# A six-layer attention and gated-MLP kernel: the rounding of the value output, its low part, and the weight remainders change engines and places

## The chip, the cores and the metric

The kernel runs on one core of a Trainium2 chip. The metric is the time of one execution in microseconds, as the median of several runs. The core has five engines that run their own instruction streams in order and wait for each other by semaphores: TensorE (PE in the rows; its weight loads are PEld), VectorE (DVE), ScalarE (ACT), GpSimd (POOL) and SyncE (SP), which issues the DMAs here.

## What is computed

`x` has 16 sequences of 256 tokens with 128 channels. A layer norm and a small causal linear attention are added to it first. Then, on another layer norm of it, come six layers, and most of the time lies there. Each layer is

```python
for i in range(DEPTH):                      # 6
    x = attn_layer(shift_tokens(x), Wqkv[i], q_scale[i], k_scale[i], Wo[i]) + x
    x = ffn_layer(shift_tokens(x), ln_g[i], ln_b[i], W1[i], b1[i], W2[i], b2[i]) + x

def attn_layer(x, Wqkv, qs, ksc, Wo):
    q, k, v = split(x @ Wqkv)               # 16 heads of 64
    q = l2norm(q) * qs;  k = l2norm(k) * ksc
    q, k = rotary(q, scale), rotary(k, 1 / scale)
    out = local_attention(q, k, v)          # windows of 32, looking one window back
    return out @ Wo

def ffn_layer(x, g, bln, W1, b1, W2, b2):
    a, gate = split((layernorm(x) * g + bln) @ W1 + b1)
    return a * gelu(gate) @ W2 + b2
```

All of it is float32.

## The kernel before, in words

**Split products.** A projection with near-float32 accuracy is made of three matmuls on rounded (fp32r) operands: `hi*hi + hi*lo + lo*hi`. For this each operand is rounded (`_hi`, by ScalarE) and the remainder `raw - hi` formed (`_lo`). It concerns the input `xs`, the value output `OT` (the attention's output, transposed), the normed `xn`, and the weights `wqkv`, `wo`, `w1`.

**Slots.** The six layers run as one software pipeline. A slot handles one sequence ("batch") of one layer, and there are 16 slots a layer, 96 in all. In slot n the projections (`proj`, eight chunks of 512 columns for q and k, and `v`, four) are made for batch n (lag 0), rope, transposes (`tr`) and attention scores for n-1 (lag 1, written with one '), the end of attention and the output projection for n-2 (lag 2, ''), the MLP for n-3 (lag 3, '''). `pipeline` calls `body` for each slot, `run_slots` runs through one engine's row of the table `ORDER` and calls the step for each word. So the order on each engine is written out by hand in that table, and only semaphores relate the engines. Names of steps: `proj` and `v` (projections), `sums` (squares' sums), `rsqrt` (ten small VectorE instructions that give the reciprocal roots for the q and k norms and for the layer norm at once), `add` and `norm` (GpSimd: sum of the rope parts, multiplication with the reciprocal root), `tr` (transpose into `b_trA`, copied to qT or kT), `qk` (scores into `b_sim`), `mk` (mask put back), `pt` (transpose of the probabilities), `pv` (product with V), `ot` (transpose of its result), `wo`, `x1`, `mean`, `var`, `ln` (layer norm), `xl` (GpSimd: `xn_lo`), `w1.0` to `w1.2`, `w2`. The four units of attention of a batch have numbers 0 to 3.

**The value output.** `pt` and `ot` share one PSUM bank, `b_trB` (its order is `TRB_ORDER`; `trB_free` is TensorE's wait for it). After `ot.u` ScalarE copies the bank to `OT` (L920, step `ot`), and that frees the bank. A second ScalarE step, `oh` (L930), rounds `OT` into `OT_hi`, and GpSimd (step `ol`, L1022) forms `OT_lo = OT - OT_hi`. `wo` (L743) waits for all four `ot_lo_done`.

**Layer edges.** At an edge the weights change under the running pipeline. ScalarE rounds the raw weights (`w_a`, L824, in three thirds of q, k and v; `w_cs`, from L969, for `wo`, the layer norm, `w1` and the rest), GpSimd forms the remainders (`w_a` L1043, together with the scaled rotary table `rotary_scaled`; `w_low`, L1031 for `wo` and L1034 for `w1`). `EDGE` says behind which word of the table a third is done; the words `wc` and `wd` stand in the table and act only in the slots in which their weights change. In the table `wd.0''` and `wd.1'''` are GpSimd's last words, behind `norm.5`. SP loads the raw weights of the next layer at once, by 20 DMAs (`load_weights` from `loads`), ahead of the slot of the layer's fourth batch; its other DMAs in a slot are `xres`, two for `xraw`, the store of x, and ten that place V.

## Time and profile before

| | us |
|---|---|
| median of 3 runs | 3533.07 |
| lowest, highest | 3528.24, 3535.49 |
| the profiled execution | 3529.75 |
| its span | 3527.9 |

The mean granted TensorE clock of the profiled execution is 0.974 of full speed. The busy shares are: TensorE 93%, its weight loads 77%, VectorE 85%, ScalarE 77%, GpSimd 70%. Matmuls are pipelined and their ends are modelled, so a TensorE that shows as busy is not one at its peak. Shares are means over stages: a prologue of some 360 us with the linear attention, the pipeline, and its short end. "Releaser" in a row is who ended a wait, "issue" is time in which an engine waited for nothing that the profile shows.

### The profile page before, as it was taken

The page shows a single profiled execution, that of the slowest core. Times are in us where ns is not written, and L with a number is a line of the kernel's source. Part 1 is how long each engine was busy: PE and PEld are TensorE (multiplying, and loading weights), DVE is VectorE, ACT ScalarE, POOL GpSimd, SP SyncE. Part 2 cuts the span into 40 slices and gives each one's busy share as a digit, 9 for nine tenths or more (in the row PEclk, how much of TensorE's full clock was granted, in tenths as well). Part 3 has the DMA queues.
Part 4 walks back from the last instruction along what each step waited for, and adds up shares of the span by engine and source line. Part 5 has one row for each costly group of instructions (what it writes and reads, how often), then busy time and mean ns, then how long its engine had stood idle before and what let it go on. Part 6 is the DMA issues. An engine that isn't in the chain of part 4 may idle for free.

```text
span 3527.9 us, 154148 instructions
## 1 busy us (share of the span) xinstructions
PE 3292.8 (93%) x64868; PEld 2708.3 (77%) x64868; DVE 3003.9 (85%) x5981; ACT 2708.9 (77%) x5023; POOL 2460.6 (70%) x2131
## 2 busy tenths in 40 slices
PE   5867999999899999899999899999899999999997
PEld 2325788887788887788887788887788888788886
DVE  7988898888788888788898788988788988888984
ACT  2015788888788888788888788888788888788884
POOL 1435678778677778677777677777677777777772
PEclk9998999999999999999999999999999999999998
DMA  2002333333333333433332433332423332323333
GB/s 86 12 27 52 91 84 80 69 77 82 90 85 71 70 85 76 95 74 68 85 84 63 105 71 75 85 82 59 107 65 84 84 76 66 76 66 85 84 80 83
DMA packets 186849, 268.07 MB, mean 76 GB/s; under 512 B 31671, under 2 KB 89909, under 8 KB 185397
## 3 DMA queue, kind: packets, MB, share of 16 engines
q1 hardware_dynamic: 186164, 258.24, 32.6%
q8 instruction: 516, 8.45, 1.0%
q14 instruction: 169, 1.38, 0.1%
HBM read 22.30 MB, written 4.19 MB: 8 GB/s over the span
## 4 chain that ended last, share of the span: by engine, by line
PE 61%; DVE 14%; issue 12%; POOL 8%; ACT 3%; SPq 1%; DVEq 0%; DMA 0%; POOLq 0%; ACTq 0%
PE bank L681 9%; PE bank L694 8%; PE obank L728 6%; PE bank L657 6%; PE bank L659 4%; PE bank L658 4%; PE bank L738 4%; PE bank L791 3%; POOL qn L1014 3%; POOL qn L1008 3%; PE bank L746 2%; PE bank L747 2%; PE bank L748 2%; PE bank L782 2%; PE bank L784 2%
## 5 line engine op out<-in xcount | busy, mean ns | idle before, releaser
L1014 POOL TENSOR_TENSOR qn<-qn,rinv 128x512 f32<-128x512 f32 x768 | 785.6, 1043 | 663.3 <-DVE rinv L1282 663.3
L1008 POOL TENSOR_TENSOR qn<-ropec,ropes 128x512 f32<-128x512 f32 x768 | 990.6, 1313 | 67.8 <-DVE ropes L1234 67.8
L879 ACT ACTIVATE sq<-bank 128x512 f32<-128x512 f32 x768 | 460.0, 599 | 179.1 <-PE bank L659 162.2
L1233 DVE TENSOR_TENSOR ropec<-bank,rots 128x512 f32<-128x512 f32 x768 | 524.2, 683 | 62.9 <-ACT sq L879 56.4
L1242 DVE TENSOR_REDUCE ss<-sq 128x8 f32<-128x512 f32 x768 | 520.1, 678 | 52.4 <-ACT sq L879 46.2
L1234 DVE TENSOR_TENSOR ropes<-bank,rots 128x512 f32<-128x512 f32 x768 | 522.5, 680 | 0.0
L1022 POOL TENSOR_TENSOR OT_lo<-OT,OT_hi 128x512 fp32r<-128x512 f32 x384 | 488.6, 1284 | 31.2 <-ACT OT_hi L930 30.7
L681 PE MATMUL bank<-ident,qn 128*128 128x128 f32 x3072 | 483.0, 280 | 12.6 <-ACT qT L897 7.1
L694 PE MATMUL bank<-kT,qT 64*32 64x64 f32 x24576 | 422.9, 218 | 10.5 <-ACT bank L903 8.0
L694 PEld LDWEIGHTS bank<-kT,qT 64*32 64x32 f32 x24576 | 360.7, 107 | 84.5 <-issue 32.0
L681 PEld LDWEIGHTS bank<-ident,qn 128*128 128x128 f32 x3072 | 340.5, 141 | 96.9 <-issue 45.5
L657 PE MATMUL bank<-wqkv_hi,xs_hi 128*128 128x512 f32 x768 | 361.8, 471 | 16.5 <-POOL wqkv_lo L1043 9.3
L728 PE MATMUL obank<-V,PT 64*32 64x65 f32 x24576 | 352.3, 227 | 8.7 <-issue 8.2
L914 ACT ACTIVATE PT<-bank 128x512 f32<-128x512 f32 x384 | 230.3, 600 | 127.9 <-PE bank L704 127.8
L728 PEld LDWEIGHTS obank<-V,PT 64*32 64x32 f32 x24576 | 289.0, 106 | 45.0 <-issue 44.3
L1288 DVE TENSOR_REDUCE mx<-bank 128x8 f32<-128x512 f32 x384 | 262.4, 683 | 70.2 <-PE bank L694 69.7
L659 PE MATMUL bank<-wqkv_hi,xs_lo 128*128 128x512 f32 x768 | 306.6, 399 | 0.0
L658 PE MATMUL bank<-wqkv_lo,xs_hi 128*128 128x512 f32 x768 | 305.2, 397 | 0.0
L1304 DVE TENSOR_TENSOR On<-obank,rs 128x512 f32<-128x512 f32 x384 | 265.5, 691 | 13.5 <-DVE rs L1299 0.2
L1293 DVE TENSOR_TENSOR Pr<-bank,mx 128x512 f32<-128x512 f32 x384 | 265.5, 691 | 13.2
L920 ACT ACTIVATE OT<-bank 128x512 f32<-128x512 f32 x384 | 231.2, 602 | 36.7 <-POOL OT_lo L1022 31.3
L897 ACT ACTIVATE qT<-bank 128x512 f32<-128x512 f32 x384 | 229.6, 598 | 37.9 <-PE bank L681 36.9
(155 smaller groups left out, 7802.3 us busy)
## 6 DMA issues: line engine op xcount, KB each, us to landing
V<-Vt SPq DMA_DIRECT2D x576, 260.0 KB
V<-Vt SPq DMA_DIRECT2D x192, 130.0 KB
V<-Vt SPq DMA_DIRECT2D x192, 65.0 KB
xres<-X SPq DMA_DIRECT2D x96, 128.0 KB, 2.1
X<-x SPq DMA_DIRECT2D x96, 128.0 KB, 2.1
wqkv_raw<-L_ffn_Wqkv SPq DMA_DIRECT2D x6, 1536.0 KB
xraw<-X SPq DMA_DIRECT2D x97, 64.0 KB, 2.1
xraw<-X SPq DMA_DIRECT2D x97, 63.8 KB, 2.0
```

The source lines that it names most:

```text
L657: pe.matmul(o, xs_hi[:, rows], wqkv_hi[:, cols], start=True, stop=False)
L659: pe.matmul(o, xs_lo[:, rows], wqkv_hi[:, cols], start=False, stop=True).then_inc(proj_full.sem, 1)
L681: mm = pe.transpose(b_trA[:, j * P:(j + 1) * P], qn[:, c, j * P:(j + 1) * P], ident[:])
L694: mm = pe.matmul(b_sim[w * WIN:(w + 1) * WIN, col:col + 2 * WIN], qT[64 * par:64 * par + 64, m, q0:q0 + WIN], kT[64 * par:64 * par + 64, m ...
L728: mm = pe.matmul(obank[w * WIN:(w + 1) * WIN, slot, j * 65:j * 65 + 65], PT[rows, u % 2, j * P + w * WIN:j * P + (w + 1) * WIN], V[rows, w ...
L879: act.activation(sq[:, c % 2, :], b_proj[n % 2][:], ACT.Square).then_inc(squared.sem, 1)
L1008: pool.tensor_tensor(qn[:, c, :], ropec[:, c % ROPE_RING, :], ropes[:, c % ROPE_RING, :], ALU.add).then_inc(rope_sum.sem, 1)
L1014: pool.tensor_tensor(heads8(qn[:, c, :]), heads8(qn[:, c, :]), rinv[:, 8 * c:8 * c + 8].unsqueeze(2).broadcast_to([P, 8, DH]), ALU.mult).t ...
L1022: pool.tensor_tensor(OT_lo[unit], OT[:, u % 2], OT_hi[unit].bitcast(F32), ALU.subtract).then_inc(ot_lo_done.sem, 1)
L1233: dve.tensor_tensor(halves(ropec[:, c % ROPE_RING, :]), raw, table(t, 2 * kind), ALU.mult)
L1234: dve.tensor_tensor(halves(ropes[:, c % ROPE_RING, :]), raw[:, :, ::-1, :], table(t, 2 * kind + 1), ALU.mult).then_inc(roped.sem, 1)
L1242: dve.tensor_reduce(ss[:, 8 * c:8 * c + 8], heads8(sq[:, c % 2, :]), AX.X, ALU.add).then_inc(ss_done.sem, 1)
```

## The change

The value output. ScalarE no longer copies the bank to `OT`; its step `ot` rounds the bank straight into `OT_hi`. The step `oh` is gone. `ol` has moved from GpSimd to VectorE and subtracts `OT_hi` from the bank itself. So the bank is free when `ot_lo_done` is raised, and TensorE's `trB_free` waits for that.

The weights. `wd.1'''` stands behind `add.3` and `wd.0''` behind `add.7`, both ahead of GpSimd's norms of the slot. The thirds have other places in `EDGE`, and the rotary table is scaled with the second third instead of the first. SP loads the weights in six parts, in the slots of six successive batches (g = 4 to 9), each ahead of the placement of V, and the Wqkv load is in three DMAs, so there are 22.

The table. All four rows are new. TensorE's slot now begins at `proj.0`; `w1.0` and `pv.2` stand at the end of the slot before, which is the same place in the cycle. Six norms in front of the slot's end have become four, with `norm.4` to `norm.7` in the next slot. `ln.0` stands ahead of `v.3` instead of behind it on TensorE, and `xn`, `xn_hi` (the step `ln`) are ahead of `v.3` on ScalarE.

```diff
     "pool": """
-        add.0 norm.6' norm.7' ol.0'' add.1 add.2 ol.1'' ol.2'' ol.3'' add.3 add.4 add.5 add.6 norm.0 norm.1
-        xl.0'' norm.2 add.7 norm.3 norm.4 norm.5 wd.0'' wd.1''' """,
+        add.0 norm.4' norm.5' norm.6' add.1 add.2 norm.7' add.3 wd.1''' add.4 add.5 add.6 add.7 wd.0'' norm.0 norm.1 xl.0''
+        norm.2 norm.3 """,
...
-        EDGE = {"act": {"last": {("proj", 7): 0, ("v", 1): 1}, "first": {("proj", 1): 2}},
-                "pool": {"last": {("add", 6): 0, ("norm", 5): 1}, "first": {("add", 2): 2}}}
+        EDGE = {"act": {"last": {("proj", 6): 0, ("proj", 7): 1}, "first": {("proj", 1): 2}},
+                "pool": {"last": {("add", 6): 0, ("add", 7): 1}, "first": {("add", 4): 2}}}
...
+                         load=(l + 1, g - 4) if 4 <= g < 10 else None)
...
+                if load is not None:
+                    loads(*load)
                 if has_a:
                     place_v(n)
...
                 if k == "pt":
                     pe.wait_ge(pt_copied.sem, pt_copied.at(batch, n + 1))
                 else:
-                    pe.wait_ge(ot_copied.sem, ot_copied.at(batch, n + 1))
+                    pe.wait_ge(ot_lo_done.sem, ot_lo_done.at(batch, n + 1))
...
             def b_ot(b, u):
                 t, par = UNIT[u]
                 act.wait_ge(trB_full.sem, trB_full.at(b, TRB_ORDER.index(("ot", u)) + 1))
-                act.wait_ge(ot_lo_done.sem, ot_lo_done.at(b, u - 1) if u >= 2 else ot_lo_done.at(b - 1, u + 3))
-                act.activation(OT[:, u % 2], b_trB[:].rearrange("p (j q) -> p j q", j=4),
-                               ACT.Copy).then_inc(ot_copied.sem, 1)
-
-            def b_oh(b, u):
-                t, par = UNIT[u]
-                act.wait_ge(ot_copied.sem, ot_copied.at(b, u + 1))
                 if u == 0:
 
                     act.wait_ge(c_full.sem, c_full.at(b - 1, 1))
                 unit = (slice(0, P), slice(4 * par, 4 * par + 4), slice(t * P, t * P + P))
-                act.activation(OT_hi[unit], OT[:, u % 2], ACT.Copy).then_inc(ot_hi_done.sem, 1)
+                act.activation(OT_hi[unit], b_trB[:].rearrange("p (j q) -> p j q", j=4), ACT.Copy).then_inc(ot_copied.sem, 1)
...
-                if k == 0:
+                if k == 1:
                     pool.wait_ge(roped.sem, roped.at(layer * NB, 8))
                     rotary_scaled(pool).then_inc(rots_done, 1)
...
+            def b_ol(b, u):
+                t, par = UNIT[u]
+                dve.wait_ge(ot_copied.sem, ot_copied.at(b, u + 1))
+                unit = (slice(0, P), slice(4 * par, 4 * par + 4), slice(t * P, t * P + P))
+                dve.tensor_tensor(OT_lo[unit], b_trB[:].rearrange("p (j q) -> p j q", j=4), OT_hi[unit].bitcast(F32),
+                                  ALU.subtract).then_inc(ot_lo_done.sem, 1)
```

The cycle of the other engines, from `proj.0`, is now, in the table's words. TensorE: `proj.0 tr.1' pt.3'' proj.1 w1.1''' tr.2' proj.2 tr.3' ot.1'' w1.2''' tr.4' proj.3 pv.3'' tr.5' ot.2'' proj.4 tr.6' w2.0''' tr.7' ot.3'' proj.5 proj.6 qk.0' wo.0'' qk.1' proj.7 v.0 mean.0'' pt.0' qk.2' var.0'' v.1 v.2 pt.1' pv.0' qk.3' pt.2' ln.0'' v.3 pv.1' tr.0 ot.0' w1.0'' pv.2'`. VectorE, from the previous batch's `qk.3''`: `qk.3'' pv.1'' xs.0 ol.0'' pv.2'' w1.0''' proj.0 sums.0 sums.1 w1.1''' proj.1 proj.2 sums.2 w1.2''' ol.1'' pv.3'' proj.3 ol.2'' sums.3 proj.4 w2.0''' sums.4 ol.3'' sums.5 qk.0' proj.5 proj.6 x1.0'' qk.1' sums.6 mean.0'' proj.7 sums.7 var.0'' qk.2' rsqrt.0 pv.0' ln.0''`. ScalarE, at the turn of the slot: `pt.2' v.2 ln.0'' v.3 | xs.0 qk.3'' tr.0' ot.0'' w1.0''' proj.0 tr.1'`.

Two places in the instruction order. On VectorE, behind the rsqrt and up to the first rope of the next batch, it is before (`rs` and `On` are the step `pv`, `mx` and `Pr` the step `qk`, `hm` is `w1`, `ropec` and `ropes` are `proj`):

```order
568 L1304 TENSOR_TENSOR On<-obank,rs 128x2x4x64
569 L1325 TENSOR_TENSOR lnt<-dlt,bank 128x256
570 L1288 TENSOR_REDUCE mx<-bank 128x8
571 L1293 TENSOR_TENSOR Pr<-bank,mx 128x512
572 L1299 RECIPROCAL rs<-obank 128x8
573 L1304 TENSOR_TENSOR On<-obank,rs 128x2x4x64
574 L1221 TENSOR_TENSOR xs_lo<-xraw,xs_hi 128x256
575 L1299 RECIPROCAL rs<-obank 128x8
576 L1304 TENSOR_TENSOR On<-obank,rs 128x2x4x64
577 L1330 SCALAR_TENSOR_TENSOR hm<-bank,vec,gel 128x256
578 L1233 TENSOR_TENSOR ropec<-bank,rots 128x512
579 L1234 TENSOR_TENSOR ropes<-bank,rots 128x512
```

and on VectorE now:

```order
648 L1328 TENSOR_TENSOR lnt<-dlt,bank 128x256
649 L1291 TENSOR_REDUCE mx<-bank 128x8
650 L1296 TENSOR_TENSOR Pr<-bank,mx 128x512
651 L1302 RECIPROCAL rs<-obank 128x8
652 L1307 TENSOR_TENSOR On<-obank,rs 128x2x4x64
653 L1224 TENSOR_TENSOR xs_lo<-xraw,xs_hi 128x256
654 L1218 TENSOR_TENSOR OT_lo<-bank,OT_hi 128x4x128
655 L1302 RECIPROCAL rs<-obank 128x8
656 L1307 TENSOR_TENSOR On<-obank,rs 128x2x4x64
657 L1333 SCALAR_TENSOR_TENSOR hm<-bank,vec,gel 128x256
658 L1236 TENSOR_TENSOR ropec<-bank,rots 128x512
659 L1237 TENSOR_TENSOR ropes<-bank,rots 128x512
```

The first of the four subtractions has come in between `xs_lo` and `pv.2`; the others stand further on, behind `w1.2`, `proj.3` and `sums.4`.

On GpSimd, at the layer edge at which `w1` changes, it is before:

```order
247 L1008 TENSOR_TENSOR qn<-ropec,ropes 128x512 x4
248 L1014 TENSOR_TENSOR qn<-qn,rinv 128x512 x2
249 L1026 TENSOR_TENSOR xn_lo<-xn,xn_hi 128x256
250 L1014 TENSOR_TENSOR qn<-qn,rinv 128x512
251 L1008 TENSOR_TENSOR qn<-ropec,ropes 128x512
252 L1014 TENSOR_TENSOR qn<-qn,rinv 128x512 x3
253 L1034 TENSOR_TENSOR w_lo<-w_raw,w_hi 128x682
254 L1008 TENSOR_TENSOR qn<-ropec,ropes 128x512
```

and now:

```order
194 L1010 TENSOR_TENSOR qn<-ropec,ropes 128x512
195 L1016 TENSOR_TENSOR qn<-qn,rinv 128x512 x3
196 L1010 TENSOR_TENSOR qn<-ropec,ropes 128x512 x2
197 L1016 TENSOR_TENSOR qn<-qn,rinv 128x512
198 L1010 TENSOR_TENSOR qn<-ropec,ropes 128x512
199 L1030 TENSOR_TENSOR w_lo<-w_raw,w_hi 128x682
200 L1010 TENSOR_TENSOR qn<-ropec,ropes 128x512 x4
201 L1016 TENSOR_TENSOR qn<-qn,rinv 128x512 x2
202 L1022 TENSOR_TENSOR xn_lo<-xn,xn_hi 128x256
```

`w_lo` stood behind the six norms that follow the rsqrt, and stands now among the rope sums ahead of them.

## Rows read from the trace of the kernel before

**Rows 1.** The page: busy time, share of the span and instructions of each engine.

```profile
PE 3292.8 (93%) x64868; PEld 2708.3 (77%) x64868; DVE 3003.9 (85%) x5981; ACT 2708.9 (77%) x5023; POOL 2460.6 (70%) x2131
```

**Rows 2.** Busy us of each engine in one interior slot, granted clock, DMA share, GB/s.

```profile
1599.30:1631.20 31.90, 31.79 (x670) 26.88 (x670) 28.54 (x60) 27.50 (x52) 24.00 (x21) 1.00 0.34 78
```

**Rows 3.** Waits of the whole span: engine, line, releaser; us, times, longest.

```profile
PEld bank L768 <- DVE rinv L1282: 47.5, 90, 2.5
...
PE bank L782 <- POOL w_lo L1034: 33.9, 5, 6.8
...
PE bank L657 <- POOL wqkv_lo L1043: 9.3, 5, 1.9
...
SPq L488 <- PE obank L728: 1764.4, 95, 28.2
```

**Rows 4.** TensorE's timeline: the first and the last ln between which 91 slots lie.

```profile
433.53 0.71 PE L768 MATMUL bank<-ident,rinv 128*128 128x128 f32 x4
...
3448.45 0.71 PE L768 MATMUL bank<-ident,rinv 128*128 128x128 f32 x4
```

**Rows 5.** Windows as in rows 2, at one layer edge.

```profile
1434.00:1441.00 7.00, 7.00 (x93) 6.03 (x94) 2.58 (x6) 4.00 (x7) 0.00 (x0) 0.65 0.01 2
...
1455.00:1462.00 7.00, 7.00 (x219) 6.06 (x218) 6.66 (x14) 4.95 (x11) 2.06 (x2) 1.00 1.05 305
...
1469.00:1476.00 7.00, 6.10 (x118) 5.49 (x110) 3.45 (x5) 3.63 (x7) 5.91 (x6) 0.50 0.12 36
```

**Rows 6.** Waits at the same edge, from 1466 to 1504.

```profile
PE bank L674 <- issue: 2.6, 1, 2.6
```

**Rows 7.** ScalarE's timeline in one slot: start, length, instruction (us).

```profile
1536.49 0.60 ACT L954 ACTIVATE xn<-lnt,vec 128x256 f32<-128x256 f32 x1 [0.39 <-issue]
1537.18 0.42 ACT L957 ACTIVATE xn_hi<-xn 128x256 fp32r<-128x256 f32 x1
1537.51 0.40 ACT L873 ACTIVATE xs_hi<-xraw 128x256 fp32r<-128x256 f32 x1
...
1538.75 0.59 ACT L920 ACTIVATE OT<-bank 128x512 f32<-128x512 f32 x1
1539.23 0.63 ACT L908 ACTIVATE Pr<-Pr 128x512 f32<-128x512 f32 x1
1539.88 1.28 ACT L948 ACT_TABLE_LOAD   x1
1541.17 0.47 ACT L948 ACTIVATE gel<-bank,vec 128x256 f32<-128x256 f32 x1
1541.54 0.59 ACT L897 ACTIVATE qT<-bank 128x512 f32<-128x512 f32 x1
1542.02 0.60 ACT L879 ACTIVATE sq<-bank 128x512 f32<-128x512 f32 x1
```

**Rows 8.** VectorE's timeline in the same slot.

```profile
1534.95 0.23 DVE L1282 SCALAR_TENSOR_TENSOR rinv<-bank,rinv 128x66 f32<-128x66 f32 x1
1535.10 0.20 DVE L1299 RECIPROCAL rs<-obank 128x8 f32<-128x8 f32 x1
...
1535.98 0.42 DVE L1325 TENSOR_TENSOR lnt<-dlt,bank 128x256 f32<-128x256 f32 x1
1537.04 0.69 DVE L1288 TENSOR_REDUCE mx<-bank 128x8 f32<-128x512 f32 x1 [0.64 <-PE bank L694]
...
1538.38 0.20 DVE L1299 RECIPROCAL rs<-obank 128x8 f32<-128x8 f32 x1
...
1539.21 0.48 DVE L1221 TENSOR_TENSOR xs_lo<-xraw,xs_hi 128x256 fp32r<-128x256 f32 x1
...
1541.68 0.48 DVE L1330 SCALAR_TENSOR_TENSOR hm<-bank,vec,gel 128x256 f32<-128x256 f32 x1
1542.65 0.69 DVE L1233 TENSOR_TENSOR ropec<-bank,rots 128x512 f32<-128x512 f32 x1 [0.49 <-ACT sq L879]
1543.26 0.68 DVE L1234 TENSOR_TENSOR ropes<-bank,rots 128x512 f32<-128x512 f32 x1
```

More of the change, by code:

```diff
@@ L316, in pipeline @@
             for l in range(DEPTH - 1):
-                loads and loads(l + 1)
                 for g in range(3, NB):
                     body(l * NB + g + 1, g, (0, 1, 2, 3), None, {2: l, 3: l},
-                         edge=("last", l + 1) if g == NB - 1 else None)
+                         edge=("last", l + 1) if g == NB - 1 else None,
+                         load=(l + 1, g - 4) if 4 <= g < 10 else None)
                 body(l * NB + NB + 1, 0, (0, 1, 2, 3), l + 1, {2: l, 3: l}, edge=("first", l + 1))
@@ L335, in build, with run_slots @@
                      "dve": {"x1": (0, 1), "mean": (2, 3), "rsqrt": (4,), "ln": (5, 6)}}
-        EDGE = {"act": {"last": {("proj", 7): 0, ("v", 1): 1}, "first": {("proj", 1): 2}},
-                "pool": {"last": {("add", 6): 0, ("norm", 5): 1}, "first": {("add", 2): 2}}}
-        def run_slots(steps, engine, n, g, lags, layer, c_layers, conv_c=None, end=0, edge=None):
+        EDGE = {"act": {"last": {("proj", 6): 0, ("proj", 7): 1}, "first": {("proj", 1): 2}},
+                "pool": {"last": {("add", 6): 0, ("add", 7): 1}, "first": {("add", 4): 2}}}
+        def run_slots(steps, engine, n, g, lags, layer, c_layers, conv_c=None, end=0, edge=None, load=None):
             for kind, i, lag in order(engine):
@@ L461, in _ @@
-            load_weights(0)
+                one = slice(layer, layer + 1)
+                if part < 3:
+                    cols = slice(part * INNER, (part + 1) * INNER)
+                    sp.dma_start(wqkv_raw[:, cols], Wqkv[one, :, cols].rearrange("l p n -> p (l n)")).then_inc(w_in_sem, 16)
+                elif part == 3:
+                    for slot in range(2):
+                        for par in range(2):
+                            src = Wo[one].rearrange("l (j s r p) n -> s r p (l j) n", j=4, s=2, r=2)[slot, par]
+                            sp.dma_start(wo_raw[slot * 64:slot * 64 + 64, 4 * par:4 * par + 4, :], src).then_inc(w_in_sem, 16)
+                elif part == 4:
+                    sp.dma_start(w1_raw[:], W1[one].rearrange("l p n -> p (l n)")).then_inc(w_in_sem, 16)
+                    for j, (f0, n) in enumerate(FFB):
+                        sp.dma_start(w2_raw[0:n, j, :], W2[one, f0:f0 + n].rearrange("l p n -> p (l n)")).then_inc(w_in_sem, 16)
+                    sp.dma_start(qks_raw[:, 0, :], q_scale[one].broadcast_to([P, DH])).then_inc(w_in_sem, 16)
+                    sp.dma_start(qks_raw[:, 1, :], k_scale[one].broadcast_to([P, DH])).then_inc(w_in_sem, 16)
+                else:
+                    col(0, ln_g[one].rearrange("l p -> p l"))
+                    col(1, ln_b[one].rearrange("l p -> p l"))
+                    col(2, b2[one].rearrange("l p -> p l"))
+                    for j, (f0, n) in enumerate(FFB):
+                        col(3 + j, b1[one, f0:f0 + n].rearrange("l p -> p l"), n)
+                        col(6 + j, b1[one, FF + f0:FF + f0 + n].rearrange("l p -> p l"), n)
@@ L463, in _ @@
+            for part in range(6):
+                load_weights(0, part)
             sp.wait_ge(ln_cp, 8)
@@ L503, in place_v, with body @@
                     move(half, 0, 0, P - WIN, slice(1, 2), WIN)
-            def body(n, g, lags, layer, c_layers, conv_c=None, end=0, edge=None):
+            def body(n, g, lags, layer, c_layers, conv_c=None, end=0, edge=None, load=None):
                 has_a, has_b, has_c, has_d = (lag in lags for lag in (0, 1, 2, 3))
@@ L539, in wrap, with loads @@
                 return (g + NB) % NB
-            def loads(layer):
-                hold(sp, sp_held, w_lo, 3 * layer)
-                hold(sp, sp_held, w_c, 4 * layer)
-                hold(sp, sp_held, w_clo, 2 * layer)
-                load_weights(layer)
+            def loads(layer, part):
+                if part == 0:
+                    sp.wait_ge(w_lo, 3 * layer)
+                    sp.wait_ge(w_c, 4 * layer)
+                    sp.wait_ge(w_clo, 2 * layer)
+                load_weights(layer, part)
             load_x(0)
-            pipeline(sp, body, loads=loads)
+            pipeline(sp, body)
             sp.wait_ge(x_stored.sem, x_stored.at(DEPTH * NB, 16))
@@ L1043, in w_a @@
                 pool.tensor_tensor(wqkv_lo[:, cols], wqkv_raw[:, cols], wqkv_hi[:, cols].bitcast(F32), ALU.subtract).then_inc(w_lo, 1)
-            steps = {"third": w_a, "add": a_add, "norm": a_norm, "ol": b_ol, "xl": c_xl, "wd": w_low}
+            steps = {"third": w_a, "add": a_add, "norm": a_norm, "xl": c_xl, "wd": w_low}
             pool.wait_ge(x1_saved, 16)
```

55 lines of the change are left out of this document (16 added, 39 removed).

## The prediction

> **What bounds the kernel now.** I read the page first, then the waits, then interior slots and layer edges by windows, then one slot by the timelines of VectorE and ScalarE. A slot is the stretch from one `ln` matmul (L768) to the next: one batch of one layer.
>
> The page gives TensorE 93% and VectorE 85% of the span [rows 1]. An interior slot takes 31.9 us: TensorE is busy for 31.8 of it, VectorE 28.5, ScalarE 27.5, GpSimd 24.0 [rows 2]. TensorE is the pacer, with one regular wait: before `ln` its weight load waits for the last step of VectorE's rsqrt, 47.5 us in 90 slots, 0.53 each [rows 3]. So TensorE alone would need about 31.4.
>
> Between the `ln` at 433.53 and that at 3448.45 lie 91 slots [rows 4]. At 31.9 they would take 2902.9; they take 3014.9. So 112 us are lost at the five layer edges and in scattered stalls, 22 a layer. What is known of them:
> - `w1.0` waits for GpSimd's `w_lo` (L1034): 33.9 us in five waits, 6.8 each [rows 3]. After it the granted clock is 0.65 over 7 us [rows 5], which is part of the stretch at 1.2 GHz instead of 2.4: some 2.4 us a time, 12 in all. Together 46.
> - While the weights load, the DMA share is 1.05 [rows 5], and then a `v` matmul waits 2.6 us for no semaphore [rows 6]; behind that the clock is 0.50 over 7 us [rows 5]. That edge loses some 6 us by it. I take 3.5 a layer as the mean, about half of this edge, so 18.
> - The first projections of a layer wait 9.3 us for `wqkv_lo` [rows 3]. With what such a hole takes from the clock I double it: 18.
> - The other 30 are ScalarE's conversions and short scattered stalls.
>
> **The change, part by part.**
>
> *Weight remainders and loads.* `wd.1` moves on GpSimd from behind norms 0 to 5 to behind `add.3`, where neither it nor the norms wait for the rsqrt. Its consumer `w1.0` comes some 20 us later, so the 46 go. The QKV thirds 0 and 1 and the rotary table now stand before the norms, in the gap in which GpSimd waits for the rsqrt; GpSimd has also lost four `OT_lo` a slot and is idle for over 12 us of a slot. The 18 go. SP's 20 weight DMAs become 22 in six slots, each part issued just ahead of the V placement. SP waits there for `pv.3` anyway: 1764.4 us in 95 slots, 18.6 each [rows 3], so the parts cost nothing, and `xres`, `xraw` and the store, queued behind them, no longer wait for 20 issues in a row. With a third of the bytes at a time the 18 of the fetch stall should go. If a part did not fit in those 18.6 us, the V placement would be late for `pv.0`, but that is read most of a slot later. Sum of the edges: -82, and between -43 (the two semaphore waits alone) and -100.
>
> *ScalarE.* Four copies of the bank into `OT` go, 0.48 to 0.59 each [rows 7]; four roundings now read the bank. ScalarE is no bound, so this counts only where its order delays somebody, below.
>
> *VectorE.* It gets four `OT_lo` subtractions a slot. No row has this one. The nearest is the rope product of the same size from a bank: 0.69 long, its successor 0.61 later [rows 8]. The output is fp32r: of two 256-element ones `xs_lo` takes 0.48 and `lnt` 0.42 [rows 8], so 0.67 is the upper bound; 0.5 the lower, since the type may cost nothing and a plain instruction may start a little earlier. I take 0.60, four make 2.4. VectorE then has 28.5 + 2.4 = 30.9 us of work in a slot of 31.9, and 1.0 of slack where it had 3.4.
>
> The Trainium skill speaks against this part: "VectorE: DVE Perf Modes", the section on the TRN2 errata, charges VectorE 120 + FD cycles from PSUM and 58 + FD from SBUF, and its rules for kernel authors advise a copy to SBUF first where many operations follow. That would be 0.06 us more for each subtraction than from `OT`, an estimate of 24 us in all. The rows say otherwise: `lnt`, with one input in a bank, is shorter (0.42) than `xs_lo`, with both in SBUF (0.48) [rows 8]. I leave it out.
>
> *The new wait, and who stands behind it.* VectorE runs in order, and its `ol.0` needs TensorE's transpose and then ScalarE's rounding. Behind it queue `pv.2`, `w1.0`, and all the ropes. Count from the start of `pv.0`, right behind the rsqrt (1535.10 in [rows 8]):
> - `lnt` starts at 0.88 [rows 8], ScalarE's `xn` 0.51 after it, `xn_hi` 0.69 after that [rows 7, 8]: 2.08.
> - `v.3` is now behind `xn_hi`: +0.33. It takes 0.48 (as `qT` to `sq`), then `xs` (0.33, as `xn_hi` to `xs`), the exp `qk.3` (0.63 less an overlap of 0.10: 0.53), `tr.0` (0.48) [rows 7]: `ot.0` starts at 4.23.
> - VectorE sees it 0.63 later, as rope after `sq` (1542.02 to 1542.65) [rows 7, 8]: 4.86.
> - Until then VectorE has `pv.0` 0.88, `lnt` 0.35, `qk.3` 1.34, `pv.1` 0.83, `xs_lo` 0.45 [rows 8]: 3.85. **It idles 1.0.**
> - `ol.0` 0.60 and `pv.2` 0.83 end at 6.29. ScalarE's gelu table starts 0.65 after `ot.0`, at 4.88, takes 1.29, and `hm` follows the gelu 0.51 later [rows 7, 8]: 6.68. The first rope follows gelu + 0.37 + 0.63: 7.17, instead of 6.68. **It idles 0.5 more.**
>
> From there to the next rsqrt I find no gap: squares, `w1.1`, `w1.2`, `ot.1` and the banks are there before VectorE comes to them, because it is late itself. So the slot becomes VectorE's loop: 30.9 + 1.5 = 32.4 to 32.5. TensorE must also fit. A bank `b_trB` now comes free only after the subtraction; `ot.2` waits for `ol.1`, which stands in VectorE's queue behind `proj.0` to `proj.2`, by about 0.7. TensorE's 31.4 + 0.7, and 0.2 for one more change between 64-row and 128-row matmuls, is 32.3, just inside. The old 0.53 at `ln` has not gone but moved to `ot.2`.
>
> So a slot grows by 0.6: 93 slots x 0.6 = +56.
>
> **Sum.** The profiled execution took 3529.75 us, span 3527.9; +56 - 82 gives 3504. It lies 3.3 under the median 3533.07 of the three runs, so for a median about **3506**. Bounds of the slot: TensorE's 31.4 (-0.5) if ScalarE keeps ahead and the subtraction is cheap, and 33.1 (+1.2) if VectorE meets a further gap.
>
> **Rivals.**
> *A. The loop is shorter than I walked.* If ScalarE gets to `ot.0` in time, VectorE has nothing to wait for and TensorE paces at 31.4 to 31.9. For it: ScalarE loses 2 us of work a slot. Against: what precedes `ot.0` on ScalarE hangs on `lnt`, not on load. 3533 - 82 = 3451, and down to 3533 - 82 - 46 = 3405.
> *B. Slower: the VectorE queue stops at `ol.1` to `ol.3` as well.* Each needs the round transpose, rounding, subtraction, and while VectorE stands there it delays the ropes that TensorE needs to free its two projection banks. For it: slack is 1.0 us and I have already spent 1.5 of waits. It decides from a slot of 32.8, where 93 x 0.9 = 84 eats the edges. At 33.1: +112 - 82, 3563.
> *C. The edges give only their two semaphore waits.* The clock dips and fetch stalls stay, as they have other causes than the weights' DMAs: -43 + 56, 3546.
>
> **How the numbers follow.** My case (slot 32.3 to 32.7, edges -65 to -100; 3480 to 3535) 0.55; A 0.20; B 0.13; C 0.12. Faster by over 0.2% (7 us, about what a measurement of this kernel can tell from no change): 0.46 + 0.20 + 0.01 + 0.02 = 0.69. Within it: 0.07 + 0.01 + 0.05 = 0.13. Slower: 0.02 + 0.11 + 0.05 = 0.18. The range 3440 to 3552 leaves out the lower half of A and the upper half of B.
>
> **What would show it.** In the profile after: interior slots of 32.4 with VectorE busy near 31; VectorE's idle time mostly before `OT_lo`, released by ScalarE's rounding; TensorE waiting before `ot.2` for `OT_lo`; no wait for `w_lo`; GpSimd near 19 us a slot; no clock of 0.5 for 7 us behind an edge. Interior slots of 31.9 or less make A right and my walk wrong; idle time before the later `OT_lo` makes B right; a `v` or `pv` matmul that still waits 2 to 3 us for no semaphore at an edge makes C right.

## The result, and the profile after

The changed kernel takes 3510.14 us in the median of nine runs (3501.38 to 3518.92), the kernel before in the same comparison 3528.71 (3524.31 to 3535.49). The ratio is 0.9946, 95% interval 0.9931 to 0.996: faster by half a per cent. 3506 was predicted, as 27 us less than the 3533.07 of the three runs before; measured against 3528.71 it is 18.6 us less. The profiled execution has a span of 3507.2 us and a mean granted clock of 0.983.

The page of the kernel after: busy time, share of the span and instructions of each engine, against [rows 1].

```profile
PE 3306.6 (94%) x64868; PEld 2705.1 (77%) x64868; DVE 3272.9 (93%) x6365; ACT 2510.8 (72%) x4639; POOL 1989.4 (57%) x1747
```

VectorE has 269 us more than before. An undisturbed interior slot, from `ln` to `ln` (now L777), by the columns of [rows 2]:

```profile
2236.58:2268.99 32.41, 32.10 (x672) 27.03 (x670) 31.37 (x64) 25.50 (x47) 19.08 (x17) 1.00 0.35 77
```

It has grown from 31.9 to 32.4, and GpSimd has come down to 19. The two `ln` matmuls that answer to [rows 4], and the windows between them, of before and then of after:

```profile
428.23 0.71 PE L777 MATMUL bank<-ident,rinv 128*128 128x128 f32 x4
...
3424.12 0.71 PE L777 MATMUL bank<-ident,rinv 128*128 128x128 f32 x4
```

```profile
433.53:3448.45 3014.92, 2925.62 (x60970) 2472.64 (x60971) 2602.91 (x5370) 2528.23 (x4702) 2245.24 (x1956) 0.99 0.36 79
```

```profile
428.23:3424.12 2995.89, 2936.09 (x60973) 2468.79 (x60971) 2859.50 (x5734) 2341.72 (x4337) 1798.99 (x1592) 1.00 0.36 80
```

The 91 slots take 19.0 us less, which is the whole gain. Part of it is the clock. Before, 12 stretches of 3.4 to 10.2 us in these slots have a granted clock of 0.50, 72 us together; after, there are two of 3.4 us. One of the two:

```profile
1310.30:1313.70 3.40, 3.40 (x58) 2.55 (x58) 3.09 (x12) 1.17 (x3) 3.40 (x5) 0.50 0.02 5
```

At 31.88 and 32.43 a slot, undisturbed slots make 2901 and 2951 us of it, +50. What lies above them, at the edges and in scattered stalls, was 114 and is 45. An undisturbed slot is no longer the usual one: the median of the 91 is 31.92 before and 32.75 after.

VectorE's timeline in the interior slot (start, length, instruction; in brackets idle time and who ended it). It answers to [rows 8].

```profile
2236.44 0.20 DVE L1302 RECIPROCAL rs<-obank 128x8 f32<-128x8 f32 x1
...
2237.33 0.42 DVE L1328 TENSOR_TENSOR lnt<-dlt,bank 128x256 f32<-128x256 f32 x1
...
2239.83 1.20 DVE L1224 TENSOR_TENSOR xs_lo<-xraw,xs_hi 128x256 fp32r<-128x256 f32 x1
2241.26 0.69 DVE L1218 TENSOR_TENSOR OT_lo<-bank,OT_hi 128x512 fp32r<-128x512 f32 x1 [0.22 <-ACT OT_hi L932]
2241.86 0.20 DVE L1302 RECIPROCAL rs<-obank 128x8 f32<-128x8 f32 x1
2242.10 0.69 DVE L1307 TENSOR_TENSOR On<-obank,rs 128x512 f32<-128x512 f32 x1
2243.04 0.48 DVE L1333 SCALAR_TENSOR_TENSOR hm<-bank,vec,gel 128x256 f32<-128x256 f32 x1 [0.26 <-ACT gel L950]
2243.53 0.69 DVE L1236 TENSOR_TENSOR ropec<-bank,rots 128x512 f32<-128x512 f32 x1
...
2249.69 0.68 DVE L1218 TENSOR_TENSOR OT_lo<-bank,OT_hi 128x512 fp32r<-128x512 f32 x1
```

`OT_lo` waits for ScalarE's rounding and starts 4.82 us behind the start of `pv.0` at 2236.44, and the first rope 7.09 behind it. Apart from these two waits, of 0.22 and 0.26, VectorE has none left in this slot. ScalarE's timeline there, the chain that these waits hang on; it answers to [rows 7]:

```profile
2237.83 0.60 ACT L956 ACTIVATE xn<-lnt,vec 128x256 f32<-128x256 f32 x1
2238.52 0.42 ACT L959 ACTIVATE xn_hi<-xn 128x256 fp32r<-128x256 f32 x1
2238.85 0.58 ACT L895 ACTIVATE Vt<-bank 128x512 f32<-128x512 f32 x1
...
2240.63 0.59 ACT L932 ACTIVATE OT_hi<-bank 128x512 fp32r<-128x512 f32 x1
2241.24 1.28 ACT L950 ACT_TABLE_LOAD   x1
2242.53 0.47 ACT L950 ACTIVATE gel<-bank,vec 128x256 f32<-128x256 f32 x1
```

TensorE's timeline where `ot.2` waits:

```profile
2248.93 0.86 PE L737 MATMUL obank<-V,PT 64*32 64x65 f32 x64
2249.72 0.66 PE L690 MATMUL bank<-ident,qn 128*128 128x128 f32 x4
2250.51 0.63 PE L747 MATMUL bank<-ident,On 128*128 128x128 f32 x4
```

`ot.2` (L747) starts 0.79 behind `tr.5`, just after `OT_lo` ends at 2250.37. It starts 0.15 behind that end in the median of the 96 slots too. Without the wait the distance is 0.49 (e11, below). So TensorE loses 0.30 here in an undisturbed slot, though these matmuls show as busy.

Waits of the whole span, against [rows 3]:

```profile
DVE hm L1333 <- ACT gel L950: 38.5, 94, 3.0
...
DVE OT_lo L1218 <- ACT OT_hi L932: 30.0, 97, 1.1
...
PE bank L703 <- issue: 14.5, 28, 1.2
...
PE bank L747 <- DVE OT_lo L1218: 5.3, 21, 0.9
...
PEld bank L777 <- DVE rinv L1285: 3.1, 3, 2.5
```

The waits for `w_lo` and `wqkv_lo` are gone, and so are 87 of 90 waits for the rsqrt. New are 28 waits in `qk` (L703) for nothing that the profile shows. The wait of `ot.2` (L747) shows in 21 slots only; in the others it is inside matmuls that are counted as busy.

### The profile page after: what moved, and what is told of

Same layout as the page of the kernel before. It is cut to its first block, busy times and chain, and to the rows that moved or that the text cites. A ratio compares the mean times of both kernels' runs of the same rounds, so it can differ in the third digit from the quotient of the medians.

```text
span 3507.2 us, 153391 instructions
## 1 busy us (share of the span) xinstructions
PE 3306.6 (94%) x64868; PEld 2705.1 (77%) x64868; DVE 3272.9 (93%) x6365; ACT 2510.8 (72%) x4639; POOL 1989.4 (57%) x1747
## 4 chain that ended last, share of the span: by engine, by line
PE 69%; DVE 13%; issue 10%; ACT 5%; POOL 1%; SPq 1%; DMA 0%; DVEq 0%; POOLq 0%; ACTq 0%
PE bank L703 10%; PE bank L690 7%; PE obank L737 6%; PE bank L713 4%; PE bank L747 4%; PE bank L666 4%; DVE ropes L1237 3%; PE bank L668 3%; PE bank L667 3%; PE bank L800 3%; PE bank L755 3%; PE bank L681 3%; DVE ropec L1236 2%; PE bank L683 2%; PE bank L682 2%
## 5 line engine op out<-in xcount | busy, mean ns | idle before, releaser
L1010 POOL TENSOR_TENSOR qn<-ropec,ropes 128x512 f32<-128x512 f32 x768 | 978.6, 1287 | 939.1 <-DVE ropes L1237 939.1
L1016 POOL TENSOR_TENSOR qn<-qn,rinv 128x512 f32<-128x512 f32 x768 | 802.2, 1066 | 270.6 <-DVE rinv L1285 270.6
L888 ACT ACTIVATE sq<-bank 128x512 f32<-128x512 f32 x768 | 449.2, 601 | 56.5 <-PE bank L668 44.4
L912 ACT ACTIVATE bank<-mask_f 128x512 f32<-128x512 f32 x384 | 230.8, 601 | 329.2 <-DVE Pr L1296 327.1
L703 PE MATMUL bank<-kT,qT 64*32 64x64 f32 x24576 | 436.7, 218 | 26.7 <-issue 14.5
L703 PEld LDWEIGHTS bank<-kT,qT 64*32 64x32 f32 x24576 | 371.3, 107 | 97.2 <-ACT kT L906 35.6
L690 PEld LDWEIGHTS bank<-ident,qn 128*128 128x128 f32 x3072 | 353.7, 140 | 113.6 <-issue 52.2
L737 PEld LDWEIGHTS obank<-V,PT 64*32 64x32 f32 x24576 | 271.2, 106 | 109.4 <-issue 95.8
L932 ACT ACTIVATE OT_hi<-bank 128x512 fp32r<-128x512 f32 x384 | 228.0, 594 | 161.9 <-PE bank L747 160.9
L737 PE MATMUL obank<-V,PT 64*32 64x65 f32 x24576 | 337.0, 226 | 4.8 <-issue 4.4
L1218 DVE TENSOR_TENSOR OT_lo<-bank,OT_hi 128x512 fp32r<-128x512 f32 x384 | 261.6, 681 | 30.1 <-ACT OT_hi L932 30.0
```

The lines of the kernel that those rows point to most:

```text
L690: mm = pe.transpose(b_trA[:, j * P:(j + 1) * P], qn[:, c, j * P:(j + 1) * P], ident[:])
L703: mm = pe.matmul(b_sim[w * WIN:(w + 1) * WIN, col:col + 2 * WIN], qT[64 * par:64 * par + 64, m, q0:q0 + WIN], kT[64 * par:64 * par + 64, m ...
L737: mm = pe.matmul(obank[w * WIN:(w + 1) * WIN, slot, j * 65:j * 65 + 65], PT[rows, u % 2, j * P + w * WIN:j * P + (w + 1) * WIN], V[rows, w ...
L888: act.activation(sq[:, c % 2, :], b_proj[n % 2][:], ACT.Square).then_inc(squared.sem, 1)
L1010: pool.tensor_tensor(qn[:, c, :], ropec[:, c % ROPE_RING, :], ropes[:, c % ROPE_RING, :], ALU.add).then_inc(rope_sum.sem, 1)
L1016: pool.tensor_tensor(heads8(qn[:, c, :]), heads8(qn[:, c, :]), rinv[:, 8 * c:8 * c + 8].unsqueeze(2).broadcast_to([P, 8, DH]), ALU.mult).t ...
```

## The experiments

One table for all of them. The fourth column is the time from the third to the last but two `ln` (91 slots, as above), the fifth an undisturbed interior slot, the last the number of stalls inside a burst of 64 small matmuls in the 91 slots (`qk` or `pv`: two of one burst start more than 0.49 us apart), and the sum of these distances. The last three are of the profiled execution.

| kernel | median us | ratio [interval] | 91 slots | slot | stalls, us |
|---|---|---|---|---|---|
| before | 3528.71 | | 3014.9 | 31.88 | 7, 9.8 |
| after | 3510.14 | 0.9946 [0.9931, 0.996] | 2995.9 | 32.43 | 31, 24.5 |
| e1 weight part alone | 3454.9 | 0.978 [0.976, 0.9801] | 2947.6 | 31.88 | 11, 9.7 |
| e2 `wd` alone | 3484.44 | 0.9868 [0.9846, 0.9889] | 2970.7 | 31.88 | 9, 11.5 |
| e5 `wd` and loads | 3461.05 | 0.9806 [0.9789, 0.9823] | 2953.6 | 31.88 | 9, 7.5 |
| e8 e1 and `add.7` | 3437.16 | 0.9742 [0.9725, 0.976] | 2931.1 | 31.88 | 6, 5.3 |
| e3 value part alone | 3564.82 | 1.0099 [1.0068, 1.013] | 3043.2 | 32.43 | 23, 23.1 |
| e4 after, `ol.1` earlier | 3541.01 | 1.0035 [1.0022, 1.0048] | 3024.3 | 32.58 | 37, 32.2 |
| e6 after, half subtractions | 3480.44 | 0.9865 [0.9849, 0.9881] | 2967.2 | 32.17 | 21, 19.6 |
| e7 after, `v.3` later | 3529.73 | 1.0002 [0.9991, 1.0013] | 3015.0 | 32.66 | 20, 19.6 |
| e9 e1, V placed later | 3451.82 | 0.9789 [0.9772, 0.9805] | 2943.8 | 31.9 | 10, 8.5 |
| e10 after, `pv.3` earlier | 3511.31 | 0.9957 [0.9941, 0.9974] | 2996.6 | 32.45 | 27, 23.8 |
| e11 after, no subtractions | 3474.09 | 0.9854 [0.9836, 0.9871] | 2958.3 | 32.11 | 17, 14.7 |
| e12 after, stream shifted | 3514.16 | 0.9954 [0.994, 0.9969] | 2996.4 | 32.45 | 25, 21.3 |

### The two halves apart

**e1** is the kernel before with the whole weight part (`wd.1` behind `add.3`, `wd.0` behind `add.6`, the new `EDGE`, the rotary table one third later, the loads in six parts) and nothing of the value part.

> The kernel before with the weight part of the change alone: `wd.1` and `wd.0` among the rope sums, the thirds moved, the loads in six parts. The value output stays as before. If the edges gain what the prediction says (82 us) and the value part costs the slots, the slot stays at 31.9 and the time is 3529 - 82 = 3447, within 3435 to 3460. If the value part has its own share in the gain (GpSimd relieved of four subtractions a slot), it is 3470 or more.

It measured 3454.9. **e3** is the opposite: the value part with the new table, but `wd` behind the norms, the old `EDGE` and the old loads.

```diff
-        add.0 norm.4' norm.5' norm.6' add.1 add.2 norm.7' add.3 wd.1''' add.4 add.5 add.6 add.7 wd.0'' norm.0 norm.1 xl.0''
-        norm.2 norm.3 """,
+        add.0 norm.4' norm.5' norm.6' add.1 add.2 norm.7' add.3 add.4 add.5 add.6 add.7 norm.0 norm.1 xl.0''
+        norm.2 norm.3 wd.0'' wd.1''' """,
```

> The changed kernel with the weight part undone: `wd` at the end of GpSimd's row, loads at once, thirds and rotary table at their old places (the second third behind `norm.3`, since `norm.5` is now in the next slot). Slots of 32.4 (+50 us) and the scattered stalls (+15), with most of the old edges: 3570 to 3595. If the gain was from a lighter GpSimd, it stays near 3510.

3564.82, a little under what was expected. So the weight part gains 74 us and the value part costs 36: the change is faster because of one half and in spite of the other. Together the halves would give 3491 and not 3510, and 3473 with e8 (below), which has `add.7` where the changed kernel has it, in e1's place. Most of these 37 us is counted twice, since the new table shortens the edges by itself. Take the six slots around each edge: before they lie 107 us above their undisturbed length, in e3 75, in e8 19, in the changed kernel 23. For one, with four norms instead of six ahead of it, `w_lo` is earlier in e3. In the waits of e3, against 33.9 in [rows 3]:

```profile
PE bank L781 <- POOL w_lo L1020: 18.4, 5, 3.8
```

**e2** moves `wd.1` and `wd.0` alone, **e5** adds the loads in six parts, and e1 is e5 with the thirds of QKV moved.

```diff
-        add.0 norm.6' norm.7' ol.0'' add.1 add.2 ol.1'' ol.2'' ol.3'' add.3 add.4 add.5 add.6 norm.0 norm.1
-        xl.0'' norm.2 add.7 norm.3 norm.4 norm.5 wd.0'' wd.1''' """,
+        add.0 norm.6' norm.7' ol.0'' add.1 add.2 ol.1'' ol.2'' ol.3'' add.3 wd.1''' add.4 add.5 add.6 wd.0'' norm.0 norm.1
+        xl.0'' norm.2 add.7 norm.3 norm.4 norm.5 """,
```

> The kernel before with `wd.1` and `wd.0` moved in GpSimd's row, and nothing else. The five waits for `w_lo` (33.9 us) and the clock lost behind them (12 us) go: 3483, within 3475 to 3490. If the clock dip has another cause, 3495. If the wait only moves to the norms behind it, no change.

> The kernel before with `wd` moved and the loads in six parts; thirds and rotary table as before. In the run with `wd` alone (3484) the slots behind the load bursts are still 4 to 7 us long, and one of 7.5 stands behind the first; in the run with all of the weight part they are not. So the parts give 25 us: 3459, and the thirds the rest to 3455. If the thirds had the larger share, it is 3470 or more.

3484.44 and 3461.05. Over the 91 slots `wd` gains 44.2, the loads 17.1, and some 7 more in the slot behind the first load, which lies ahead of the 91; the thirds gain 6.0. In e1 one slot at each edge was still 3.7 us over 31.88. There TensorE waits for a norm, and GpSimd does that norm behind the rotary table and a QKV third, since `add.7`, to which the third is tied, stood behind `norm.2`. The waits of e1 in that slot, 2339.3 to 2375:

```profile
PE bank L691 <- POOL qn L1024: 1.8, 1, 1.8
```

**e8** is e1 with `add.7` ahead of the norms, as in the changed kernel.

```diff
-        ... add.3 wd.1''' add.4 add.5 add.6 wd.0'' norm.0 norm.1 xl.0'' norm.2 add.7 norm.3 norm.4 norm.5
+        ... add.3 wd.1''' add.4 add.5 add.6 add.7 wd.0'' norm.0 norm.1 xl.0'' norm.2 norm.3 norm.4 norm.5
```

> The kernel before with the whole weight part (3455), and `add.7` ahead of the norms, so that the k third of `wqkv_lo`, which follows it, is done in GpSimd's wait for the rsqrt. The slot at the edge that is 3.7 us long by TensorE's wait for this third loses 3 of them, five times: 3440, within 3433 to 3447. If GpSimd then is late with the norms, 3455 or more.

3437.16, as expected, and the fastest of all, 2.6% under before and 2.1% under after. That slot is now 0.9 us over 31.88, and the 91 slots gain another 16.5. An interior slot of e8 is as long as before.

### What sets the slot of 32.4

I held that it is VectorE's loop, and that TensorE, at 31.6 of its own, has room. The rival was ScalarE's chain ahead of `ot.0`, or TensorE's `ot.2`. **e4** takes the wait of `ot.2` away, by doing `ol.1` two steps earlier on VectorE:

```diff
-        ... proj.2 sums.2
-        w1.2''' ol.1'' pv.3'' ...
+        ... proj.2 ol.1'' sums.2
+        w1.2''' pv.3'' ...
```

> The changed kernel with `ol.1` two words earlier on VectorE, ahead of `sums.2` and `w1.2`, so that it ends 0.8 us earlier and TensorE need not wait for it before `ot.2`. If VectorE's own loop sets the slot, the slot stays at 32.4 within 0.15 and the time within 3495 to 3515; TensorE's wait turns up again before `ln`. If TensorE's path through `ot.2` sets it, the slot falls to 31.8 and the time to some 3455.

It took 3541.01, 26 us over the expected range, with a slot of 32.58. The wait at `ot.2` has gone, but each slot has a new one, a projection that waits for its bank until the ropes are done:

```profile
PE bank L666 <- DVE ropes L1237: 22.9, 97, 0.8
```

Slots account for 14 of the 31 us over the changed kernel (91 x 0.15), more stalls in the bursts and at the edges for the rest. **e7** shortens ScalarE's chain ahead of `ot.0` by the copy of `v.3`, which it makes behind `proj.0` of the next slot instead:

```diff
-        xs.0 qk.3'' tr.0' ot.0'' w1.0''' proj.0 tr.1' ...
+        xs.0 qk.3'' tr.0' ot.0'' w1.0''' proj.0 v.3' tr.1' ...
...
-        wc.1'' v.3 wc.3''' """,
+        wc.1'' wc.3''' """,
```

> The changed kernel with ScalarE's copy of `v.3` taken from between `xn_hi` and `xs` to behind `proj.0` of the next slot: 0.48 us out of the chain from the rsqrt to the gelu and the first square. If this chain is part of the loop, the slot falls by 0.3 to 0.5, to some 32.0, and the time to 3465 to 3485. `proj.1` on TensorE may wait 0.3 for its bank then. If the chain is beside the loop, no change: 3510.

3529.73, a miss again, with a slot of 32.66. VectorE's waits for `OT_hi` fell to 10.2 us, but `proj.1` now waits for the copy, which frees its bank. TensorE's timeline there, and the wait of the whole span:

```profile
2060.40 0.60 PE L713 MATMUL bank<-ident,Pr 128*128 128x128 f32 x4
2061.32 0.51 PE L666 MATMUL bank<-wqkv_hi,xs_hi 128*128 128x512 f32 x1 [0.32 <-ACT Vt L895]
```

```profile
PE bank L666 <- ACT Vt L895: 33.1, 95, 1.0
```

`proj.1` starts 0.92 behind the start of `pt.3`, where the changed kernel has 0.36, so TensorE loses 0.56 of the slot of 32.66, and 32.1 is left. e4 and e7 have each put a new wait in place of the old one, so neither prices the old one by itself. **e6** makes each subtraction on half of its columns and leaves that part of the low product out (`OT_lo` is set to zero once, ahead of the pipeline):

```diff
-                dve.tensor_tensor(OT_lo[unit], b_trB[:].rearrange("p (j q) -> p j q", j=4), OT_hi[unit].bitcast(F32),
+                dve.tensor_tensor(OT_lo[unit][:, 0:2], b_trB[:].rearrange("p (j q) -> p j q", j=4)[:, 0:2],
+                                  OT_hi[unit].bitcast(F32)[:, 0:2],
                                   ALU.subtract).then_inc(ot_lo_done.sem, 1)
```

> The changed kernel with each `OT_lo` subtraction on half of its columns (the other half of `OT_lo` is zero: part of the low product is left out, so this is no version of the kernel, only a price). Each subtraction is 0.27 us shorter. If VectorE's loop sets the slot, the three behind the first rope count in full, the first is covered by its wait: slot 32.4 - 0.8 = 31.6, or where TensorE takes over, 31.7: 3435 to 3455. If VectorE does not set it, 32.4 and 3510.

3480.44, the third miss: most undisturbed slots are 32.17 (eight are 32.1) with 0.9 us of VectorE's work gone. `ot.2` there still starts 0.15 behind the end of `OT_lo`, 0.04 later than it would without. In all three TensorE is left with 32.1, and **e11**, in which the subtractions are nearly gone, puts the question to it alone. Against e6:

```diff
-                dve.tensor_tensor(OT_lo[unit][:, 0:2], b_trB[:].rearrange("p (j q) -> p j q", j=4)[:, 0:2],
+                dve.tensor_tensor(OT_lo[unit][:, 0:1, 0:1], b_trB[:].rearrange("p (j q) -> p j q", j=4)[:, 0:1, 0:1],
```

> The changed kernel in which each of the four subtractions is made on one element of its 512 a partition, the rest of the low part staying zero, so this kernel leaves out nearly the whole low part of the value output. VectorE has some 2 us a slot less to do. With half of each subtraction the slot was 32.09 to 32.17 and TensorE's steps showed no wait but 0.04 us. Theory 1: TensorE's own sum in the new order is 32.1 (it was 31.5 in the old one, against the 31.6 that I reckoned with), so the slot stays at 32.1 and the time at 3475 to 3485. Theory 2: VectorE or ScalarE still set the slot with half the subtractions: it falls to 31.6 to 31.9 and the time to 3430 to 3460.

3474.09, within 1 us of its first theory. Interior slots of e6 (one of the shortest) and e11:

```profile
2289.80:2321.88 32.08, 31.91 (x672) 26.99 (x671) 30.48 (x63) 25.31 (x47) 19.06 (x17) 1.00 0.36 77
```

```profile
2254.27:2286.38 32.11, 31.94 (x673) 27.10 (x671) 29.65 (x64) 25.41 (x47) 19.07 (x17) 1.00 0.35 78
```

VectorE has 0.8 us less to do in the second, and the slot stays within 0.06. The place of `ot.2` in e11:

```profile
2267.41 0.66 PE L690 MATMUL bank<-ident,qn 128*128 128x128 f32 x4
2267.90 0.60 PE L747 MATMUL bank<-ident,On 128*128 128x128 f32 x4
```

0.49 from start to start: no wait. **So TensorE takes 32.1 in the new order, whatever VectorE does.** In the changed kernel VectorE's loop adds 0.3 to that, by way of `ot.2`; in e4 it adds 0.5 by way of a projection's bank, in e7 ScalarE adds 0.5 by way of the copy of `v.3`.

Not all of the 32.1 is work. In the new order only `proj.2` stands between `tr.2` and `tr.3`, which share the bank `b_trA`, and `tr.3` may start only when ScalarE has copied `tr.2` out of it. All engines in e11 there:

```profile
2262.35 0.60 PE L690 MATMUL bank<-ident,qn 128*128 128x128 f32 x4
...
2262.99 0.60 ACT L906 ACTIVATE kT<-bank 128x512 f32<-128x512 f32 x1
...
2263.26 0.40 PE L668 MATMUL bank<-wqkv_hi,xs_lo 128*128 128x512 f32 x1
...
2263.70 0.42 PEld L690 LDWEIGHTS bank<-ident,qn 128*128 128x128 f32 x4 [0.48 <-issue]
2263.73 0.63 PE L690 MATMUL bank<-ident,qn 128*128 128x128 f32 x4
```

ScalarE's copy ends at 2263.59, and `tr.3` starts 0.14 later. It stands 0.47 behind the projection's last matmul, where 0.23 is usual, so 0.24 is lost in this round trip. In the changed kernel `tr.3` comes as late, 1.02 behind the start of `proj.2`. The profile names no releaser for it ("issue"). That it is the copy is read from the order and these rows: in the 93 such slots of each of five kernels with the new order `tr.3` starts 0.14 behind the copy's end, as `ot.2` starts 0.15 behind the end of `OT_lo`. No run took the copy away. It leaves 31.87 for TensorE's work.

### The stalls in the bursts

Between before and after the stalls inside bursts went from 7 to 31, and each of these 38 ends 2.2 to 3.0 us behind the start of a 16 KB transfer on the instruction queue, while it begins anywhere from 0.1 to 2.4 behind it. Over all 14 kernels every one ends so; in two of them, behind a load of all weights at once (one in e2, one in e3), the transfer starts only when the stall has begun. Of the 31 of the changed kernel 13 lie in `qk.1`, 11 in `qk.3` and 7 in `pv`; two of the 7 before, with half of the 9.8 us, follow a weight load. One of the stalls, in `qk.1` of slot 30, in TensorE's timeline, with that queue's row for 1369.8 to 1370.3:

```profile
1371.32 1.08 PE L703 MATMUL bank<-kT,qT 64*32 64x64 f32 x58
1372.70 0.31 PE L703 MATMUL bank<-kT,qT 64*32 64x64 f32 x6 [0.30 <-issue]
```

```profile
q8 instruction: 1, 0.02, 14.7%
```

The suspicion fell on the DMAs that place V, which run at a DMA share of 1.0 until just when `qk.1` starts, in the changed kernel 1 us longer. **e9** delays them by 1 us in e1, **e10** brings them forward by 0.8 in the changed kernel.

```diff
                 sp.wait_ge(o_full.sem, o_full.at(n - 1, 4))
+                if n:
+                    sp.wait_ge(trB_full.sem, trB_full.at(n - 1, TRB_ORDER.index(("ot", 2)) + 1))
```

> The kernel with the whole weight part and the old value output, and in it SP places V one TensorE step later: it waits for the transpose ot.2 as well, which comes 1.0 us behind the end of pv.3. In the kernel with the weight part alone the placement keeps the DMA share at 1.0 until 23 us behind ln, and the burst qk.1 runs from 22.9 to 23.9; in the changed kernel the placement lasts until 24 and qk.1 runs from 23.2 to 24.3, and 16 of its 31 stalls inside bursts lie in qk.1, with an instruction fetch started 21.4 to 22.9 us behind ln. Theory 1: a fetch that must share the DMA engines with V comes too late for the burst, so it is the later placement that makes the stalls: some 8 to 15 stalls in qk.1 instead of none, 3465 to 3475 us. Theory 2: the stalls come from TensorE's new order, in which fetch and burst fall together whatever the DMAs do: no stall in qk.1, 3453 to 3458.

```diff
-        ... w1.2''' tr.4' proj.3 pv.3'' tr.5'
+        ... w1.2''' tr.4' pv.3'' proj.3 tr.5'
```

> The changed kernel with pv.3 ahead of proj.3 on TensorE instead of behind it, so that V is placed 0.8 us earlier. Theory 1 (the placement's DMAs make the fetches late): the stalls in qk.1 go from 16 to under 5, some 8 to 10 us, so 3498 to 3504. Theory 2 (TensorE's order makes them): they stay, 3508 to 3513. The interior slot should stay at 32.4 either way, since proj.3 ends later by 0.8 but VectorE has ol.1 and pv.3 ahead of it; if it has not, a slot grows by up to 0.3 and the time to 3530.

Neither moved it: no stall in `qk.1` in e9 (10 in all, none in `qk`), 27 in e10, 16 of them in `qk.1` (13 by the same count in the changed kernel, where the expectations say 16). The suspicion falls. **e12** leaves the pipeline as it is and only lengthens TensorE's stream ahead of it, by 126 instructions:

```diff
-            for m in range(3):
+            for m in 22 * (0, 1, 2):
                 mm = pe.transpose(b_sim[:, m * P:(m + 1) * P], la_w_rows[:, m, :], ident[:])
```

> The changed kernel with 63 more transposes on TensorE far ahead of the pipeline (three transposes of the prologue are made 22 times), so that its instruction stream stands 126 instructions further on, and nothing in the pipeline is changed. In the traces every stall inside a 64-row burst stands 2.0 to 3.2 us behind the start of a 16 KB transfer on the instruction queue, and in the changed kernel and in the two with shortened subtractions and with pv.3 early, qk.1 stalls in the same slots (27, 30, 33, 36, 39, 42) at the same matmul of the 64 (62, 58, 56, 53, 51, 48). Theory 1: what decides is where the borders of these pieces of the stream fall among the bursts; then the stalls of these slots and places go, others come 63 matmuls away, and their number changes, to anything between 8 and 35; the time changes by the sum, 3495 to 3515 us, with 8 us of it for the added transposes. Theory 2: what decides is time in the slot (transfers, the steps around), not the place in the stream: qk.1 still stalls in these slots, 25 to 35 stalls, 3515 to 3522 us.

In slot 30 the burst now runs through, and in slot 58 one stands still behind its 56th matmul:

```profile
1373.03 1.10 PE L703 MATMUL bank<-kT,qT 64*32 64x64 f32 x64
...
2297.68 0.99 PE L703 MATMUL bank<-kT,qT 64*32 64x64 f32 x56
2299.03 0.32 PE L703 MATMUL bank<-kT,qT 64*32 64x64 f32 x8 [0.37 <-issue]
```

The places have moved: `qk.1` stalled in slots 27, 30, 33, 36, 39, 42 at matmul 62, 58, 56, 53, 51, 48, and now does in slots 8, 11, 14, 17, 20, 23 at 58, 56, 52, 50, 47, 45, and again in 55 to 67 at 59 to 48. The number did not change much, 25 for 31. So a stall is bound to a place in the instruction stream and ends with a transfer of it. That the place is the border of such a piece, late in a burst, fits both but is not seen itself. How many there are goes with TensorE's order: 6 to 11 in the six kernels with the old order, 17 to 37 in the eight with the new. Why a border late in `qk.1` stalls in the new order and not in the old, where `wo` stands ahead of it as well, is open.

## Why the prediction was right, and where its steps were not

**The time** was right within 4 us. The change was forecast as -27 and is -18.6; half of that distance is hidden because the kernel before came out 4 us lower in nine runs than in the first three, which is luck. The two terms of the sum held: slots +50 where +56 was put, edges -84 where -82 was. The third, +15 from stalls, was not in it. Inside the term of the slots some steps were wrong and cancelled.

**The walk along VectorE's queue** held to 0.1 us: `ol.0` 4.82 behind `pv.0` (4.86 predicted), the first rope 7.09 (7.17), no wait from there to the next rsqrt, the subtraction 0.60 from start to start and 0.68 long. The loop came out at 32.41, for 32.4 to 32.5, but by other parts. Of work there was 31.37, of which 0.7 is the longer `xs_lo`; the idle time was 0.22 + 0.26 instead of 1.5, most of the first microsecond having gone into that longer `xs_lo`; and 16 pauses of 0.03 us between short instructions, 0.55 in all, were missing from my sum. They stand in the kernel before too. That these parts, each off by 0.2 to 0.6, add up to 32.4 is luck.

**The subtraction** was put at 0.60 from rows of which one was misread. I took `xs_lo`'s 0.48 as the price of an instruction with both inputs in SBUF. But it stands beside a GpSimd multiplication there (last section); in e3 and in e12 one `xs_lo` has GpSimd idle beside it and takes 0.42 and 0.41, like `lnt`. So the rows show the bank as no dearer than SBUF, and not as cheaper. The 0.60 held.

**TensorE's own sum** was the step that failed. I took the 0.53 us that the weight load waited before `ln` [rows 3] from the slot of 31.9, and got 31.4. But a weight load can wait while the matmuls before it still run. Before the old `ln` the matmuls themselves stand apart by:

```profile
1598.64 0.40 PE L673 MATMUL bank<-wqkv_lo,xs_hi 128*128 128x512 f32 x1
1598.88 0.40 PE L674 MATMUL bank<-wqkv_hi,xs_lo 128*128 128x512 f32 x1
1599.34 0.38 PE L768 MATMUL bank<-ident,rinv 128*128 128x128 f32 x1
```

0.46 where 0.24 is usual from such a matmul to the next, so 0.22 was lost, and TensorE's old work was 31.66, not 31.4. The 0.2 that I added for the new order was right in size (31.87 against 31.66); that it comes from one more change between kinds of matmul, as I put it, no run shows. What I did not look for is the round trip of `tr.3` through ScalarE, 0.24. So in place of 31.6 stands 32.1, and the wait of `ot.2` is 0.3 where 0.7 was predicted. The two add up to much the same (32.3 and 32.4), again by luck, so the forecast of the slot did not suffer; the expectations that were built on the 31.6 did (e4, e6, e7).

**The edges.** `wd` gained 44 (46 predicted, its wait and the clock together), the loads 17 (18) and 7 more in the slot behind the first load. The thirds gained 22.5 where I had put 18: 6.0 with `EDGE` alone (e1), and 16.5 once `add.7`, to which the k third is tied, stood ahead of the norms (e8), which is what the prediction describes. I doubled a wait of 9.3 us for what it might cost at the clock. In the five slots with that wait, 26 us above their undisturbed length before, the clock does fall to 0.50 for 3.4 us in four, and TensorE waits another 6.9 us ahead of `wo`; both are gone in e8. 44 + 17 + 22.5 is 84, and what is left, 30 of the 114, is the 30 that the prediction left.

**Not foreseen** were the stalls in the bursts. The edges and slots alone would give 2981 us for the 91 slots; it is 2996. The stalls account for that: 24.5 us instead of 9.8. In the 61 slots away from the edges they can be told from everything else: these lie 6.8 us above their undisturbed length before, with 2.8 us of stalls, and 21.7 after, with 21.0.

**The rivals.** A, the shorter loop, is excluded by the interior slot. B, later subtractions that stop VectorE, did not occur: 93 of the 97 waits are at `ol.0`. C is excluded by the clock and the missing waits: at the edges a `v` and a `pv` matmul waited 2.6 us each before, and now no matmul of the 91 slots waits more than 1.4. But its idea, stalls that stay for a reason that has nothing to do with the weights' DMAs, is what took 15 us in another place.
